# A six-stage decoder on one core: mixture-of-experts routing moved into the attention stage ahead of it, a transpose copy handed to VectorE, and three reorderings

## What is computed

```python
xn = (x - mu) * rsqrt(var + EPS) * gamma + beta
logits = einsum('btd,ed->bte', xn, router_w)        # E = 8 experts
probs = softmax(logits / TEMP); w, idx = top_k(probs, 2)
h = silu(einsum('btd,edf->betf', xn, W1)); y = einsum('betf,efd->betd', h, W2)
out = einsum('bte,betd->btd', wdense, y) + res
```

## Time and profile before

| | us |
|---|---|
| median of three runs (lowest, highest) | 4176.59 (4171.93, 4178.02) |
| the profiled execution | 4185.04 |
| its span, first to last instruction | 4183.2 |
| PE, DVE, ACT, POOL busy | 3380.4, 2143.3, 1949.6, 935.2 |

### The profile page before, as it was taken

The page is one execution under the profiler, slowest core; times in us unless marked ns, Lnnn a source line. Parts: engine busy times, 40 slices in busy tenths (PEclk is TensorE's granted clock), DMA queues, the critical chain, the costliest instruction groups (busy, mean ns, idle before and its releaser), DMA issues. The chain is left out here.

```text
span 4183.2 us, 72856 instructions
## 1 busy us (share of the span) xinstructions
PE 3380.4 (81%) x25752; PEld 2491.4 (60%) x25752; DVE 2143.3 (51%) x6691; ACT 1949.6 (47%) x4754; POOL 935.2 (22%) x724
## 2 busy tenths in 40 slices
PE   6888888767697788888898879999996429999970
PEld 3565565567586466666665657777775316666650
DVE  4777777679676445555545534555544301111116
ACT  5778777633421555655556536566653101111110
POOL 0000000034000766666766400000000440000014
PEclk9999999978798899999999989999998569999995
DMA  2000000010201222221221110000002520001113
GB/s 74 12 12 18 12 12 8 12 46 16 94 1 45 56 55 58 57 54 46 60 57 49 40 43 25 20 17 17 22 12 87 193 75 31 30 29 31 31 38 107
DMA packets 120192, 178.06 MB, mean 43 GB/s; under 512 B 23776, under 2 KB 75424, under 8 KB 119328
## 3 DMA queue, kind: packets, MB, share of 16 engines
q1 hardware_dynamic: 113696, 156.61, 12.7%
q0 software_dynamic: 6144, 16.79, 1.3%
HBM read 90.88 MB, written 32.11 MB: 29 GB/s over the span
## 5 line engine op out<-in xcount | busy, mean ns | idle before, releaser
L893 ACT ACTIVATE a_t<-a_t,a_neg 128x512 f32<-128x512 f32 (+3 forms) x1024 | 643.0, 634 | 9.4 <-DVE a_neg L1070 7.9
L720 PE MATMUL a_T<-ident,a_t 128*128 128x128 f32 x3328 | 503.8, 286 | 76.7 <-ACT a_pT L884 58.7
L884 ACT ACTIVATE a_pT<-a_T 128x512 f32<-128x512 f32 (+3 forms) x896 | 415.9, 502 | 309.9 <-PE a_T L720 308.9
L720 PEld LDWEIGHTS a_T<-ident,a_t 128*128 128x128 f32 x3328 | 381.1, 145 | 267.5 <-issue 234.7
L1065 DVE CUSTOM_DVE_ANT_0 a_t<-a_A,a_table 128x384 f32<-128x384 f32 (+3 forms) x512 | 221.4, 487 | 343.9 <-PE a_A L697 341.7
L1065 DVE CUSTOM_DVE_ANT_0 a_t<-a_A,a_decay 128x512 f32<-128x512 f32 x512 | 323.0, 687 | 98.9 <-PE a_A L685 98.7
L2076 PE MATMUL experts_H<-ex_w,experts_xgT 128*128 x576 | 268.9, 610 | 40.3 <-ACT experts_xgT L2103 40.3
L2126 DVE COPY experts_y<-experts_Y 128x256 f32<-128x256 f32 x72 | 30.6, 425 | 511.4 <-PE experts_Y L2064 511.4
L921 POOL TENSOR_TENSOR a_rsin<-a_rawswapped,a_sin 128x512 f32<-128x512 f32 x128 | 166.7, 1302 | 558.2 <-DMA a_rawswapped<-a_raw 544.4
L1065 DVE CUSTOM_DVE_ANT_0 x_t<-x_A,x_table,x_mx 128x512 f32<-128x512 f32 x256 | 177.0, 748 | 169.2 <-PE x_A L697 169.0
L2064 PE MATMUL experts_Y<-ex_w,experts_hT 128*128 x1152 | 260.5, 379 | 1.0 <-DVE experts_hT L2135 1.0
(11 more groups left out here) (277 smaller groups left out, 7022.2 us busy)
## 6 DMA issues: line engine op xcount, KB each, us to landing
a_rawswapped<-a_raw SPq DMA_DIRECT2D x512, 64.0 KB, 2.0
a_invrep<-a_inv_dram SPq DMA_DIRECT2D x64, 256.0 KB, 3.9
ex_w<-in_f_w_dram SPq DMA_DIRECT2D x16, 1024.0 KB, 13.6
moe_sent<-route_zeros SPq DMA_DIRECT2D x1, 9216.0 KB, 29.9
experts_xg<-moe_sent SPq DMA_DIRECT2D x72, 128.0 KB, 2.2
moe_results<-experts_y SPq DMA_DIRECT2D x72, 128.0 KB, 1.7
a_xin<-x_all SPq DMA_DIRECT2D x16, 512.0 KB, 3.0
x_xin<-x_all SPq DMA_DIRECT2D x16, 512.0 KB, 4.1
```

What stands on the lines that cost most here:

```text
L720: mm = pe.transpose(bank[:, kt, :], t_of(u, j, kt * P, (kt + 1) * P), sh.ident[:])
L884: nc.scalar.activation(to, of, ACT.Copy).then_inc(t_empty, 1)
L893: nc.scalar.activation(t_of(u_e % U, j, 0, n), t_of(u_e % U, j, 0, n), ACT.Exp, bias=neg[:, slot, j:j + 1], scale=SCALE, accum_out=total[: ...
```

## The change

**Routing goes into x1.** A new class `Routing` holds the buffers. In x1, from batch 2 on, VectorE runs `choose(b-2)` two pieces per head in steps 0 to 4, and `locate(b-2)` in steps 6 and 7; GpSimd runs `send(b-2)`; PE appends two counting products to the last "y". Batch 6 is done in the tail of x1, batch 7 in the routing stage. The router product is now 32 multiply-reduces of 256 elements on VectorE per batch, not a matmul. A row's place no longer depends on how many rows the other experts get: each expert has an area of 4096 rows in `sent` (33,792 rows in all), cleared by 33 DMAs of 1 MB from GpSimd in the first attention; each tile's row is looked up with a register on SP. Five loads (1.3 MB) join those of x1.

```diff
+    def choose(self, dve, nv, x_all, steps, met, b):
+        for qt in range(QT):
+            ins = nv.bn_stats(self.stats[:, qt, :], x_all[:, b * QT + qt, :])
...
+        for _ in rsqrt_columns(nv, steps, self.mv[:, :, 1], self.scratch):
+            yield
...
+        if b:
+            wait_apart(dve, met, (self.arrived, 16 * self.G * b))
+        for qt in range(QT):
+            ins = nv.tensor_scalar(self.xn[:, qt, :], x_all[:, b * QT + qt, :], self.mv[:, qt, 0:1],
...
+        for _ in range(6):
+            yield
+        wait_apart(dve, met, (self.rows, b + 1))
+        for qt in range(QT):
+            for e in range(NE):
+                ins = nv.tensor_tensor_reduce(self.junk[:, e % 2, :], self.xn[:, qt, :], self.router[:, e, :], 1.0, 0.0,
+                                              ALU.mult, ALU.add, self.logit[:, qt, e:e + 1])
+                if e % 2:
+                    steps.mark(ins)
+                if e % 2:
+                    yield
+                if e % 2:
+                    steps.settle()
...
+    def locate(self, nv, steps, b):
+        for g in range(self.G):
+            yield
+            steps.settle()
+            steps.mark(nv.tensor_tensor(self.upto[:, g + 1, :], self.upto[:, g, :], self.count[:, 1, g, :], ALU.add))
...
+        nv.tensor_copy(self.place[:, b * self.G:(b + 1) * self.G], self.picked[:]).then_inc(self.placed, 1)
...
+    def send(self, pool, met, b):
+        wait_apart(pool, met, (self.normal, b + 1))
+        nc.gpsimd.tensor_tensor(self.xn[:], self.xn[:], self.gamma[:].unsqueeze(1).to_broadcast(wide),
+                                ALU.mult).then_inc(self.scaled, 1)
...
+        wait_apart(pool, met, (self.placed, b + 1))
...
+        for g in range(G):
+            pool.indirect_dma_start(self.sent, ...
```

```diff
@@ VectorE's step in attention @@
+                route = x1 and b >= 2
+                if route and s == 0:
+                    routed[1] = ro.choose(dve, nc.vector, sh.x_all, routed[0], (ready, N_READY), b - 2)
+                if route and s == 6:
+                    routed[1] = ro.locate(nc.vector, routed[0], b - 2)
                 for j in range(5):
+                    if route and s != 5:
+                        advance(routed[1], 2)
...
+            if x1:
+                advance(ro.locate(nc.vector, routed[0], B - 2))
@@ GpSimd in attention @@
+            if a0:
+                for i in range(SLOTS // CLEAR):
+                    if i % 4 == 0 and i // 4 < B:
+                        pool.wait_ge(xt_done, (i // 4 + 1) * DT)
+                    pool.dma_start(ro.sent[i * CLEAR:(i + 1) * CLEAR, :].rearrange("(p r) d -> p (r d)", p=P),
+                                   zeros[:]).then_inc(ro.cleared, 16)
+            if x1:
+                for b in range(B - 1):
+                    ro.send(pool, (ready, N_READY), b)
@@ route: SyncE has the 16 weight loads alone; GpSimd @@
+            ro.send(pool, (ready, 1), B - 1)
+            pool.wait_ge(ro.arrived, 16 * GROUPS)
```

```diff
-            items = {"a0": ([], [0], [1], []), "a1": ([], [0, 1], [2, 3], []), "x1": ([], [0, 1], [2, 3], [4])}[kind]
+            items = {"a0": ([], [0], [1], []), "a1": ([0, 1], [2, 3], [], []), "x1": ([], [0, 1], [2, 3], [4])}[kind]
...
-        found += [(1 + 2 * k if len(works) > 1 else 1, work) for k, work in enumerate(works)]
+        found += [(1 + k * (1 if len(works) > 2 else 2), work) for k, work in enumerate(works)]
...
-                if a0 and s < U and (own if u_t >= 0 else prev):
+                if not x1 and s < U and (own if u_t >= 0 else prev):
                     u = u_t % U
                     wait_apart(dve, (ready, N_READY), (pv, b * U + (u_t + 1)),
                                (t_full, (b * U + u_t) * T_UNIT + (4 + T_CREDIT)))
-                    nc.vector.tensor_copy(p_tile(u, 3, 0, 4), T[(u * T_UNIT + 3) % 2][:]).then_inc(t_copied, 1)
+                    kts, bank = keys(u) // P, T[(u * T_UNIT + 3) % 2]
+                    nc.vector.tensor_copy(p_tile(u, 3, 0, kts), bank[:, 0:kts, :] if kts > 1 else bank[:, 0, :])\
+                        .then_inc(t_copied, 1)
```

```diff
                 if not first:
                     down(i - 1, 1 - parity)
+                if more:
+                    transpose_rows(1 - parity, pair + (parity + 1))
                 for half in range(2):
                     pe.wait_ge(h_act, i * 2 + (half + 1 + 2))
...
-                if more:
-                    transpose_rows(1 - parity, pair + (parity + 1))
```

More of the change, by code:

```diff
@@ L227, in attention @@
+def attention(nc, sh, kind, w, ro):
     a0, a1, x1 = kind == "a0", kind == "a1", kind == "x1"
@@ L713, in transpose_head @@
                 job = ug * T_UNIT + j
-                free = [(t_empty, job + 1)] if not a0 else \
+                free = [(t_empty, job + 1)] if x1 else \
                     [(t_copied, ug + 1)] if j == 1 else [(t_empty, ug * 3 + (2, 0, 3, 4)[j])]
@@ L876, in step @@
                 for j in range(5):
-                    if do_t and j < (3 if a0 else T_UNIT):
+                    if do_t and j < (T_UNIT if x1 else 3):
                         u = u_t % U
@@ L1007, in run @@
                     dve.wait_ge(*seg.full(turn, work))
+                    if x1 and work[1] == QT - 1 and b >= 2:
+                        routed[0].mark(nc.vector.tensor_copy(
+                            ro.count[:].rearrange("p a g e -> p (a g e)"),
+                            A[seg.bank(work)][:, D:D + 2 * Routing.G * NE]))
                     row = sh.x_all[:, b * QT - QT + work[1], :]
@@ L1090, in _ @@
             norm = []
+            routed = [ro.steps(dve, (ready, N_READY)), None] if x1 else None
             def begin():
@@ L1953, in _ @@
-            steps.link(nv.tensor_scalar(n, upto[:, GROUPS - 1, :], float(P - 1), None, ALU.add))
+            nv.memset(ro.scratch[:], 0.0).then_inc(ready, 1)
+            dve.wait_ge(ready, 1)
+            steps = ro.steps(dve, (ready, 1))
+            advance(ro.choose(dve, nv, sh.x_all, steps, (ready, 1), B - 1))
+            dve.wait_ge(counted, 1)
+            steps.mark(nv.tensor_copy(ro.count[:].rearrange("p a g e -> p (a g e)"), C[:]))
+            advance(ro.locate(nv, steps, B - 1))
+            wide = [P, BQ, NE + TOP]
@@ L1954, in _ @@
+            nv.tensor_copy(total[:, :, 0], ro.packed[:, :, NE])
+            steps.link(nv.tensor_copy(small[:, 0, :], ro.upto[:, 0, :]))
+            nv.tensor_tensor(ro.packed[:], ro.packed[:], total[:].to_broadcast(wide), ALU.subtract).then_inc(shifted, 1)
+            n, tiles, ends, other, base, gap = [small[:, i, :] for i in range(6)]
+            steps.link(nv.tensor_tensor(n, n, ro.first[:], ALU.subtract))
+            steps.link(nv.tensor_scalar(n, n, float(P - 1), None, ALU.add))
             steps.link(nv.tensor_copy(small_i[:, 0, :], n))
@@ L1969, in _ @@
-            steps.link(nv.tensor_reduce(picked[:], sums, AX_X, ALU.add))
-            nv.tensor_copy(place[:], picked[:]).then_inc(ready, 1)
+            steps.link(nv.tensor_tensor(base, tiles, ends, ALU.subtract))
+            steps.link(nv.scalar_tensor_tensor(out=base, in0=base, scalar=float(P), in1=ro.first[:],
+                                               op0=ALU.mult, op1=ALU.add))
+            steps.link(nv.tensor_tensor(gap[:, 0:NE - 1], base[:, 1:], base[:, 0:NE - 1], ALU.subtract))
@@ L1977, in _ @@
-            steps.link(nv.tensor_copy(expert_of[:], iota[0:1]))
-def experts(nc, sh, w1, w2, w_in, expert_of, sent, results):
+            nv.tensor_reduce(row[:, 0], past[:, 0], AX_X, ALU.add)
+            steps.link(nv.tensor_tensor(past[:, 1], past[:, 0], gap[0:1, 0:NE - 1].unsqueeze(1).to_broadcast(shape),
+                                        ALU.mult))
+            nv.tensor_copy(expert_of[:], row[:, 0])
+            steps.link(nv.tensor_reduce(row[:, 1], past[:, 1], AX_X, ALU.add))
+            steps.link(nv.scalar_tensor_tensor(out=row[:, 1], in0=ro.iota[0:1], scalar=float(P), in1=row[:, 1],
+                                               op0=ALU.mult, op1=ALU.add))
```

379 lines of the change are left out of this document (195 added, 184 removed).

## The result

The changed kernel took 4076.95 us (median of four runs, 4074.16 to 4092.46), the kernel before 4177.31 in the same group of runs: a ratio of 0.977 (95% interval 0.974 to 0.980), 100 us less, where 89 less were forecast (4088). A later group of runs of the same two programs gave 4018.6 against 4160.3, a ratio of 0.9645 (0.962 to 0.967), 142 us less. (A group is a set of runs made beside each other.) So the first number hides errors of mine in opposite directions, and one effect that only the first group shows. The traces take it apart.

A forecast was written before the change was run, and what follows sets the result against it. TensorE bounds the experts and last attention, GpSimd's rotation the causal attention's seams, a routing chain and queued indirect DMAs the routing stage. Terms -130 + 55 + 4 + 20 - 40 + 2 = -89 us: 4176.6 to 4088, range 4010 to 4155.

The forecast's parts named there:

- Routing stage: From the last attention's last scores to the first expert tile: 130 us less, since seven of eight batches leave the stage.
- Last attention: Last attention stage: 55 us more, 9.3 us in each of six batches that carry routing; bounds 15 and 95.
- Causal attention: Causal attention stage: 20 us more, the least sure term, from earlier items and VectorE's copy; bounds -30 and 60.
- Now it stops ahead of L741 for nine: Causal attention, step 9: TensorE waits some 9 us for VectorE's late copy; with step 8, 6.9 us later, seven batches 48.
- copying terms: Causal attention: VectorE's copy of transposes costs 48 us beside the layer norm and 14 in ordinary steps.
- the size of the items: Causal attention seams: GpSimd's rotation items, given earlier, save 6.7 us at each of seven seams, 47 us; bounds 0 and 61.
- Experts: Expert stage: 40 us less, as TensorE's 39.8 us of waits for the row copy in 71 tiles go.
- First attention: First attention stage: 2 us more, for 33 MB of clearing writes in bursts of 4 MB.
- Half-rate reduces: Second rival: multiply-reduces on VectorE take 0.62 us each, step 2 of the last attention costs 10.7; 4154 us, chance 0.12.
- The weights: Rival at the routing stage: expert weights, loading at half their rate, become the bound, 36 us later; 4124 us, chance 0.09.
- VectorE's additions absorbed: Rival, both attentions: reduces fit idle time, the copy costs only ScalarE's gain; 3998 us, one alone about 4043, chance 0.24.
- Each unit waiting for the copy: Rival, causal attention: each of 128 units waits 1.7 us for VectorE's copy; slower, 4289 us, chance 0.05.

## Why the forecast was near, step by step

The forecast for the whole was right, 4088 against 4077, and that it came so near is luck: 100 us is a sum in which 36 us of a wait I had not seen stood against gains that I had put too low. Against the later group (142 us less) the forecast is 53 us short.

- **Routing stage: right, -122.5 for -130.** The chains of batch 7 came out within 2 us. The tail's additions did too: the rows were ready 13.1 us after the last scores (12.3 forecast) and locate(6) ended 52.3 after them (51.2). The step that failed is "eight issues by GpSimd at 1.27, 10.2 us. The block can't close before": the next block begins 5.9 us after the start of the last issue (3309.84 to 3315.7), and the sum has 1.3 for that. By the semaphores the last rows landed at 3312.3; what the other 3.4 us are is not shown. VectorE sat idle for 15.6 us over issues and closing. The 10.2 us at the far end, for 10.4, are luck in part: beside the weights the last rows landed 5.4 us after their issue where they took 2.3 before, and from there to SP's first load it was 2.5 us, not 5.9.
- **Last attention: right, 44.3 for 55, in the later groups.** Step 2's 5.2 us are 5.4, and the 2 us for the clock are 1.65, in step 3. The "1.3" of steps 6 and 7 and "0.6" of counting are 0.5 and 0.45. In six batches that is 48, and batch 0 is 3 us shorter in this pair. (That is its step 4: 12.2 to 13.6 us in the three traces with this stage as before, 10.6 in seven of the others and 13.5 in three; why is not shown.) The loads took 3.7 for 4. "[I]ts eight issues of a batch (10.2 us) end a whole step ahead of the next use of the row buffer: free" is the statement that failed in the first group. I asked who waits for the data, not what else happens while the issues run: 4.8 us a batch in step 7 (18.9 for 14.0) and 1.4 in step 0 of the five batches after, 36 in all.
- **Causal attention: wrong, -13 for +20.** Two steps failed. "Now it stops ahead of L741 for nine": it doesn't. (Its absence is one of the signs of being wrong that the prediction names.) The products of unit s-4 wait for the copy of unit s-4, which VectorE made a step earlier (TensorE's wait at L961 is for `u_v + 2` with a credit of one), and only the next unit's second transpose waits for this step's copy. So the late copy takes the place of a wait that was there:

```profile
1691.17 1.09 PE L922 MATMUL a_O<-a_pT,a_v 128*64 128x128 f32 x16
...
1691.84 5.46 DVE L151 TENSOR_SCALAR x_all<-x_all,a_mv,a_scratch 128x256 f32<-128x256 f32 x4
...
1697.39 0.56 DVE L1254 COPY a_pT<-a_T 128x384 f32<-128x384 f32 x1
...
1698.10 1.94 PE L901 MATMUL a_T<-ident,a_t 128*128 128x128 f32 x8 [4.33 <-DVE a_pT L1254]
```

The products ran ahead of the layer norm as before, and 4.33 us at the transposes stand where 5.25 stood at L757. Step 9 is 0.5 us longer, and steps 8 to 10 together 1.5, not 6.9. The 62 us of copying terms are 0 with the items moved, about 10 without. The other step is the size of the items: 27 us, where 47 were taken. They moved by one step, from 13 and 14 to 12 and 13, and not by two as is said ahead of the prediction and in it. Steps 0 to 2 are 7 us shorter, which is what was counted (6.7). But steps 12 and 15 are 2.6 and 2.5 us longer and step 14 only 2 shorter, 3 in all, and for these steps the sum has nothing. Why step 15 is longer is not shown.
- **Experts: right, -58.7 for -40.** The mechanism is the one named, the term was mis-sized. I took the idle time that the profile gives ahead of L2076 for the cost. In the kernel before:

```profile
3702.92 0.38 PE L2056 MATMUL experts_X<-ident,experts_xg 128*128 128x128 f32 x2
3703.86 3.70 PE L2076 MATMUL experts_H<-ex_w,experts_xgT 128*128 x8 [0.56 <-ACT experts_xgT L2103]
```

and after, between the same kinds of instructions:

```profile
3704.97 0.38 PE L2166 MATMUL experts_X<-ident,experts_xg 128*128 128x128 f32 x2
3705.18 1.04 PE L2199 MATMUL experts_HT<-ident,experts_h 128*128 128x128 f32 x8
3706.06 3.60 PE L2186 MATMUL experts_H<-ex_w,experts_xgT 128*128 x8
```

Two transposes take 0.38 us by their ends, but the next instruction starts 0.21 after their start when nothing stops it. From start to start the step was 0.94 and could be 0.21: 0.73 us a tile, and 0.10 more in L2076 itself (3.70 to 3.60). That is the 0.82 between 8.80 and 7.98.
- **First attention: right in the first pair**, 2.6 for 2, but 17 in the second. As said above, whether GpSimd's 33 clearing DMAs have a part in that is open.
- **The rivals.** Half-rate reduces: no (422 ns). The weights: no, but narrowly. The last of their loads is issued at 3350.7 and landed at 3365.4, the last rows at 3365.0, and TensorE's first product with the weights starts at 3371.0. (The prediction had the weights behind the next block's start by 46.5 us; it was 49.7.) The second rival gives 10.7 us for step 2; its own terms give 5.2 + 4.0, or 11.2 with the clock. VectorE's additions absorbed: half of it, the copy was and the reduces weren't, which would have been "about 4043"; with the experts' true size that is 4024, and the later group has 0.9645 x 4177 = 4029. Each unit waiting for the copy: no.

## What to carry over

Price an idle gap of TensorE from start to start, against the same pair of instructions where nothing stops them. For a new wait, read which unit's count it names before saying who stops; a wait on the step before was free here. And work that is "behind nothing" on its own queue, such as indirect DMAs beside a busy stage, is to be looked up where the same instructions already run beside others: there the trace of before had links 1.40 us apart, not 0.27.

## What the runs showed of the hardware

While GpSimd issued indirect DMAs, 23 semaphore increments of TensorE came 3.8 to 6.8 us after the start of their products, and VectorE's links stood 1.40 us apart instead of 0.27. This was so in the first group of runs and in none of four later ones, and there beside some of the issues, not all. The same stage of indirect gathers beside a layer norm took 119 to 120 us there and 98 to 100 elsewhere. What makes the difference between the groups stays open, and so does whether the issues cause it. It is worth 21 us to the kernel before and 57 to the changed one, more than some changes are: whoever compares two kernels has to profile both in one group.

With the expert weights still loading, the last scattered rows landed 5.4 us after their issue; in the kernel before, with the weights long there, they took 2.3.
